# Products of the identity for TensorE ahead of and between its waits, on a three-stage transformer block on one core

## The reference

```
x = x + cross_attention(norm(x), ctx, ctx)        # 16 heads, scores under a threshold masked
x = x + two_layers(norm(x))                       # each: retention with 8 heads, then a GELU feed-forward
x = x + mixture(norm(x))                          # 8 experts, top 2 of them per token

# cross attention, per batch and head
scores = Q K^T / sqrt(32);  scores = where(scores <= thr, -1e9, scores)
out = softmax(scores) V;    return out Wo^T + bo
# retention, per batch and head; q, k rotated by position
out = ((q k^T) * decay) v;  x = (swish(xn Wg) * group_norm(out)) Wo + x;  x = gelu(norm(x) W1) W2 + x
# mixture
w, i = top_2(softmax(x rw^T));  w = w / sum(w);  out = sum_i w_i * (silu(x Wg_i^T) * (x Wu_i^T)) Wd_i^T
```

## Time and profile before

| | |
|---|---|
| median of three runs | 1801.18 us |
| profiled execution | 1803.37 us, span 1801.6 us |
| mean granted clock of TensorE | 0.964 |
| TensorE busy | 1681.6 us (93%), 9152 products |
| VectorE busy | 1100.0 us (61%) |
| ScalarE busy | 855.7 us (47%) |
| GpSimd busy | 468.4 us (26%) |
| SyncE's issue of the identity's DMA | at 1.27 us |
| chain that ended last, by engine | PE 22%, DVE 2%, DMA 1% |

### The profile page before, as it was taken

One profiled execution on the slowest core, in us unless ns is written; L12 is line 12 of the kernel. 1 busy time (PEld: TensorE's weight loads), 2 busy tenths in 40 slices (PEclk: granted clock), 3 DMA queues, 4 the chain that ended last, 5 costly groups with the idle time before them and its releaser, 6 DMA issues. The chain is left out here.

```text
span 1801.6 us, 26166 instructions
## 1 busy us (share of the span) xinstructions
PE 1681.6 (93%) x9152; PEld 1437.5 (80%) x9152; DVE 1100.0 (61%) x2213; ACT 855.7 (47%) x1192; POOL 468.4 (26%) x340
## 2 busy tenths in 40 slices
PE   5999999999998599989999999999975999999997
PEld 4899999999998488768787887787864888888886
DVE  5445555555554566654336665634237999999995
ACT  3444444444443322245335222443324888888884
POOL 0344344443443244400002443300001121212221
PEclk9899999999999699989999999999976999999999
DMA  4111011001100410012224000222332334545622
GB/s 163 48 36 32 28 35 35 25 33 35 35 24 0 142 48 0 1 61 92 94 82 159 23 0 1 83 93 86 113 132 90 97 103 163 180 158 191 253 63 65
DMA packets 35216, 139.64 MB, mean 78 GB/s; under 512 B 4752, under 2 KB 5392, under 8 KB 28432
## 3 DMA queue, kind: packets, MB, share of 16 engines
q1 hardware_dynamic: 29984, 126.75, 19.8%
q0 software_dynamic: 5168, 12.06, 3.4%
HBM read 227.92 MB, written 12.85 MB: 134 GB/s over the span
## 5 line engine op out<-in xcount | busy, mean ns | idle before, releaser
L1774 DVE TENSOR_TENSOR e_w<-e_raw,e_w 128x2048 fp32r<-128x2048 f32 x138 | 311.4, 2285 | 14.3 <-ACT e_w L1635 14.3
L1635 ACT ACTIVATE e_w<-e_raw 128x2048 fp32r<-128x2048 f32 x138 | 264.1, 1917 | 46.6 <-DMA e_raw<-in_we 20.6
L81 PE MATMUL bank<-e_w,e_xT 128*128 128x512 f32 x1104 | 275.1, 399 | 1.4 <-DVE e_xT L1792 1.4
L81 PEld LDWEIGHTS bank<-e_w,e_xT 128*128 128x128 f32 x1104 | 206.9, 191 | 43.7 <-DVE e_xT L1792 1.8
L81 PE MATMUL bank<-ctx,wk 128*128 128x258 f32 x1536 | 195.4, 287 | 3.8 <-PEq L196 3.8
L81 PE MATMUL bank<-x2T,fw 128*128 128x512 f32 x768 | 191.6, 400 | 7.8 <-DVE x2T L1150 7.8
L81 PEld LDWEIGHTS bank<-ctx,wk 128*128 128x128 f32 x1536 | 189.6, 192 | 3.9 <-issue 3.9
L1357 PE MATMUL bank<-fw,hh 128*128 128x512 f32 x768 | 189.8, 396 | 2.2 <-DVE hh L1207 2.2
L81 PE MATMUL bank<-wv,ctx 128*128 128x512 f32 x768 | 189.2, 395 | 0.0
L81 PEld LDWEIGHTS bank<-x2T,fw 128*128 128x128 f32 x768 | 146.3, 192 | 41.2 <-DVE x2T L1150 8.9
L1357 PEld LDWEIGHTS bank<-fw,hh 128*128 128x128 f32 x768 | 144.0, 188 | 36.8 <-issue 2.1
(11 more groups left out here) (238 smaller groups left out, 2728.3 us busy)
## 6 DMA issues: line engine op xcount, KB each, us to landing
e_raw<-in_we SPq DMA_DIRECT2D x143, 1024.0 KB
fraw<-in_wf SPq DMA_DIRECT2D x64, 512.0 KB, 3.4
ctxraw<-in_ctx SPq DMA_DIRECT2D x32, 514.0 KB, 3.4
wraw<-in_wa SPq DMA_DIRECT2D x20, 512.0 KB, 4.8
X<-in_x SPq DMA_DIRECT2D x2, 1024.0 KB, 6.4
acc_d<-X SPq DMA_DIRECT2D x8, 256.0 KB, 9.2
xh_d<-A SPq DMA_DIRECT2D x8, 256.0 KB, 9.3
out<-acc_d SPq DMA_DIRECT2D x4, 512.0 KB, 6.4
```

The lines of the kernel that those rows point to most:

```text
L81: last = nc.tensor.matmul(out, lhs(t, a), rhs(t, b), start=start and n == 0, stop=n == len(steps) - 1)
L1635: nc.scalar.activation(w[pos][:, 0, :, :], raw[pos][:, :, :], ACT.Copy).then_inc(m["w_hi"], 1)
L1774: nc.vector.tensor_tensor(w[pos][:, 1, :, :], raw[pos][:, :, :], r(w[pos][:, 0, :, :]), ALU.subtract).then_inc(m["w_lo"], 1)
```

## The change

A new function `spin` issues n products of the identity with itself (128 x 128, f32) into the first 128 columns of a bank that nothing reads. It is called at eleven places of TensorE's order, 183 products in all: 14 and 4 around the first turns of the set-up; 16 before the last batch's turn, behind an added wait for VectorE's last threshold (`u_ok`), and 14 before its projection; 32 before and 16 behind the first turn of retention; 12 before the late turns of routing, 10 before the counting products and 34 before the table; 26 before the first group's turn and 5 behind it. No other instruction is changed, and no engine but TensorE gets or loses any.

```diff
+def spin(nc, bk, ident, n):
+
+    for _ in range(n):
+        nc.tensor.matmul(bk[:, 0:P], ident[:, :], ident[:, :], start=True, stop=True)
...
+                    spin(nc, bank[7], ident, 14)
                     for t in range(4):
                         turn(t)
+                    spin(nc, bank[7], ident, 4)
                     pe.wait_ge(w_lo, 1)
                     pe.wait_ge(xT_lo, 4)
...
                     with pe.Fori(1, NT) as it:
                         body(it, False)
+                    pe.wait_ge(u_ok, DC * NB)
+                    spin(nc, bank[2], ident, 16)
                     turn(NB - 1)
                     pe.wait_ge(oT_ok, HPC * (NB - 1))
                     attend(BPT - 1, NB - 1, None)
+                    spin(nc, bank[2], ident, 14)
                     project(NT - 1)
...
                     if layer == 0:
+                        spin(nc, bank[3], ident, 32)
                         pe.wait_ge(m["xh_ok"], 1)
                         turn(xh[0], bank[2]).then_inc(m["x_turned"], 1)
+                        spin(nc, bank[3], ident, 16)
...
                         last.then_inc(q["logit_ps"], 1)
+                    spin(nc, bank[7], ident, 12)
                     for i, t in enumerate(late):
...
                     score(len(late) - 1)
+                    spin(nc, bank[7], ident, 10)
                     pe.wait_ge(q["both_ok"], 1)
...
+                    spin(nc, bank[7], ident, 34)
                     pe.wait_ge(q["carried_ok"], 3)
...
+                    spin(nc, bank[6], ident, 26)
                     turn_x(0, 0)
+                    spin(nc, bank[6], ident, 5)
                     tiles(pe, body)
```

## The result

The changed kernel took 1791.54 us (median of five, 1790.84 to 1792.08) against 1800.62 (median of five, 1799.01 to 1801.67): a ratio of 0.9950, 95% interval 0.9936 to 0.9965. That is 9.1 us less. The forecast was 1790.5, range 1786 to 1797. The profiled execution took 1791.9 us, its span is 1790.1, and TensorE's mean granted clock rose from 0.964 to 0.979. Of 57 executions of the kernel before in this record, 56 lie between 1797.4 and 1805.9 us; the other took 4310.19 us and is left out.

The account below looks back on a forecast made before the run. TensorE was taken as busy 93% of the span, its clock low at four places near the edit. Terms 1.6 + 4.4 + 0.7 + 2.9 + 1.45 + 1.9 = 12.95 off 1803.4 gave 1790.4, forecast as 1790.5 us, range 1786 to 1797.

Parts of the forecast that it names:

- Whether identity products lift the clock: All blocks: the products count towards TensorE's clock, which returns after 3.4 to 6.0 us; otherwise 1824.5 us, chance 0.09.
- Set-up, 1.6: 14 and 4 products in the set-up: first two turns save 0.8 us, half the query's possible 1.6 another 0.8.
- Last batch, 4.4: 16 and 14 products in cross-attention's last batch: turns, attention and projection at full clock save 4.4 us (3 to 4.6).
- Entry of retention, 0.7: 32 and 16 products at retention's start: 0.8 us gets past VectorE, less 0.1 for a late turn (-0.5 to 0.85).
- nothing for luck elsewhere: The range's low end sums the terms' outer bounds, 15.8 us less, with no allowance for places outside the blocks.
- Routing, 12: 2.9: 12 products at routing's entry: turns start 1.8 us late, turns and scores run faster, net 2.9 us saved (1.5 to 3.4).
- 10: 10 products before routing's counting products, in TensorE's 3.28 us wait for VectorE's choice: 0 us (-1.0 to 0.4).
- 34: 1.45: 34 products before routing's table, inside 8.59 us of idle: the last table pieces end sooner, 1.45 us saved (0 to 1.5).
- First group, 1.9: 26 and 5 products in the first expert group: faster turn 0.5 us, ScalarE's wait for the gate product 1.40 (0 to 2).
- Rival 2: Clock rises but is late or lost between blocks, taking 6 us from the sum: 1796 us, chance 0.15.
- Rival 3: Gains do not reach the kernel's end, as 0.8 of 2.5 us at retention's entry: 1799 us, chance 0.05.
- that excess: The profiled execution's 2.2 us above the median of three runs, read as late clock returns and not subtracted again.

Follow-up runs that it names:

- narrow blocks: The change's eleven blocks at the same places and counts, each product 8 columns instead of 128; 1818.97 us against 1800.32 for the kernel before, ratio 1.0113.
- blocks of turns: The change's eleven blocks as transposes of the identity, two for each product; 1788.18 us against 1800.32 for the kernel before, ratio 0.9934.
- The parts timed alone: Three kernels, each with only some of the change's blocks, against the kernel before: set-up (ratio 0.9996), last batch (0.9996), routing and first group (0.9975).

## Why the prediction was right, point by point

- **Whether identity products lift the clock.** Right, and the term on which all hung. At 6.33 us the 28 pieces ran at half clock by their pace (6.24 us), and behind them it was up: the next eight turns took 1.11 us, where they had taken 1.94; the pieces at full clock cost 0.112 us (32 in 3.74) and at half 0.214, as predicted. The narrow blocks show the other case and its price. The rows that the prediction leaned on for this did not isolate the turns: 16 plain products of 128 columns stand among those of the earlier trace rows, and 16 of 64 columns before the rise at 1130.2. The blocks of turns alone do.
- **Set-up, 1.6.** Came as 2.57. The earlier turns gave 1.0 for the 0.8 written. For the query's 1.6 I took half, and in this profile it came whole, since the clock outlived a gap of 2.12 us. Half was the right mean, by luck: with the same code three of six profiles kept it, but where it was lost it fell ahead of the gap that the prediction weighed. A further 1.15 us came at the first key products, which got their clock 3.5 us after they began (53.2 to 56.7) instead of 6. It is not shown to be a gain of the blocks: from these products to the loop's at 100 us it was 44.43 us before and 43.29 after, and 43.1 to 43.4 in the three profiles without blocks in the set-up.
- **Last batch, 4.4.** Came as 4.21. Every step is in the rows: 3.74 and 3.29 us of blocks inside the idle time, attention 2.02, projection 3.06, and 0.33 us of wait left before it. The size hangs on the profile of before, which was of the slow kind here (14.63 us; a profile without blocks took 11.54).
- **Entry of retention, 0.7.** Came as 0.27. The gain behind VectorE was well sized (0.94 for 0.8); the step that failed is "0.1 to 1.3 late; ... 1.0 of that costs nothing". The clock rose 6 us after the block began, the slow end of my range, the turn was ready to start at 601.9 and started at 603.47, 1.55 late. ScalarE stood 0.2 us for it, so it cost some 0.3 where I wrote 0.1; another 0.4 was ScalarE's second weight split, which came later behind its DMA.
- **Untouched pauses, not a term at all.** The prediction added "nothing for luck elsewhere", and the elsewhere gave back 2.8 us. This is the largest gap in the sum: with everything shifted by 8 us, the clock also rose at other moments in pauses that nobody touched (2.0 and 4.4 us into the two products of the second layer before, 4.8 and 5.9 after). 2.0 of the give-back lies in the second layer's transition, where before was one of three fast profiles in ten, 1.1 at that layer's start.
- **Routing, 12: 2.9.** Came as 2.66: turns 2.1 late (1333.76, where 1337.08 less 5.43 was possible) for 1.8, scores 2.74 us for 5.13. **10:** 0, as predicted; the block ran at half clock in part (3.64 us). **34: 1.45**, came as 1.1, since the clock was down from 1353.8, in the last of the table's products (2.49 us for 3.60; at full clock I had counted about 2).
- **First group, 1.9.** Came as 2.0; the gate product took 3.04 us, and ScalarE's activation followed its table load at once. But the step "26 x 0.223 = 5.8 us lie in the 7.08 us of the gather" failed: the block took 7.35 us, and the wait would have ended after 4.7, since the gather landed in 3.5 us instead of 5.8. The turn was held for 2.2 us, about what the faster gather had given; that the term came right is luck.
- **Rival 2** (the clock is late or lost between blocks) happened in small: low stretches of 3.4 us at the counting products and the table, at a cost of some 0.4 us there and a part of the 2.2 at the first group, not 6. **Rival 3** did not: 0.27 instead of 2.5 at one place, but each other gain reached the end in the profile; in the times the set-up and the last batch, each alone, show none that can be told from nothing.
- **The sum and the median.** 12.95 predicted, 11.5 between the two profiled executions, 9.1 between the medians. The profiled execution of before lay 2.75 us above the median of five, and that of after at its own median (1791.9 and 1791.54). I had refused to subtract that excess again, as being clock time that the change would win; that was right in effect, as the second layer's luck went the other way. That 1790.5 came within 1.0 us owes something to errors that offset each other: 2.1 us not predicted and won in the set-up, 2.8 lost in the layers.
- **What stays open:** how often the last batch's blocks are worth 4.2 us and how often 1.1, which would have to explain 4.3 us in the profile and hardly 1 in the times, and whether the set-up and the last batch add up only in company. The parts timed alone (0.7, 0.7 and 4.5 us, by their ratios) sum to 5.9; the change without retention's entry, which is these parts together, measured 9.9 by its ratio (8.4 by medians). The intervals are 1.6 to 2.3 us either way for each, so that this is at the edge of what they can tell.

## What to carry to other kernels

Here TensorE's clock fell in waits, and where the work behind a wait was on the path, dummy work in it paid, if it was of the kind that lifted the clock (at 128 columns the kernel took 9.1 us less, at 8 columns 18.7 more) and ended before the wait did, and it paid more once it covered nearly all the pauses: eleven blocks gave 0.5%, the same with blocks at seven more places and one longer gave 1.3%. That is what to try elsewhere. A wait can get shorter once the blocks are there (the first group's gather landed in 3.5 us for 5.8), and a block may run in part at half clock (the 26 before that group took 7.35 us, and 6.05 at full clock), so look in the profile after the change whether anything behind a block starts late. The block behind the barrier at retention's entry started slow and ran over (10.27 us); with one behind the last product before the barrier too, the clock was still up and it took 7.38. Judge such a change by several executions: the last batch's blocks were worth 4.2 us against three profiles without them and 1.1 against a fourth.

## What the runs showed of the hardware that was not expected

- Full-width turns lifted TensorE's clock as ordinary products did (up 5.6 us after they began, in the change 6.0; 1788.18 us for the kernel against 1791.54), while 8-column products left it at 0.50 through 13.5 us in which TensorE did nothing else and did not pause (598.1 to 611.6).
- The delay of the rise varied with the moment, for the same kind of work: in the changed kernel 6.0 us for the block at retention's entry (593.36 to 599.4) and 4.4 for routing's (1328.94 to 1333.3), and 3.5 for the first keys (53.2 to 56.7), which needed 6 before.
- The same code kept the clock over a gap of 2.12 us of standing in one profile (query 3.01 us) and in three others lost it at 16.4 to 17.1, ahead of that gap and behind pauses of only 1.41 and 0.40 us (query 4.66 in the set-up alone).
- A gather of the same bytes landed in 5.8 or 5.9 us in the four profiles without blocks ahead of the first group, and in 3.5 to 4.3 in the eight with 128-column ones.
- The 8 us of spread between executions of one program (1797.4 to 1805.9 us) went with the clock: of the 51 executions of the kernel before beside the experiments, the 15 with a mean granted clock of 0.967 took 1797.4 to 1799.4 us, the 4 with 0.963 took 1802.5 to 1805.9.
